# Graph layer and experts: the last token block's messages in two column halves on a bias from ScalarE, one rank product and two shared products moved

## What is computed

```python
# graph layer on the layer-normed x
HW = norm(x) @ W
x = x + relu(segment_sum(edge_w[:, None] * HW[dst], src, 1024) + bias)
# expert layer: the input is normed, then routed; 64 experts, top 2
xt = norm(x)
scores = sigmoid(xt @ Wg.T + bg)
w, idx = top_k(scores, 2);  w = w / w.sum()
nx = norm(xt)
h = silu(nx @ W1p[e] + b1p[e]) * (nx @ W3p[e] + b3p[e])     # hidden 256
y = sum over the two experts of w * (h @ W2[e] + b2[e])
z = (silu(nxs @ Ws1 + bs1) * (nxs @ Ws3 + bs3)) @ Ws2 + bs2  # shared expert, nxs = nx * gs + bs
x = x + y + z
```

## Time and profile before

| | us |
|---|---|
| median of 3 runs | 431.51 (431.15 to 432.36) |
| profiled execution | 432.0 |
| its span, first to last instruction | 430.2 |
| TensorE busy | 398.4 (93% of the span) |
| VectorE / GpSimd / ScalarE busy | 213.2 / 174.1 / 156.9 |

### The profile page before, as it was taken

The page is one execution under the profiler, slowest core; times in us unless marked ns, Lnnn a source line. Parts: engine busy times, 40 slices in busy tenths (PEclk is TensorE's granted clock), DMA queues, the critical chain, the costliest instruction groups (busy, mean ns, idle before and its releaser), DMA issues.

```text
span 430.2 us, 6405 instructions
## 1 busy us (share of the span) xinstructions
PE 398.4 (93%) x1898; PEld 207.4 (48%) x1899; DVE 213.2 (50%) x696; ACT 156.9 (36%) x387; POOL 174.1 (40%) x275
## 2 busy tenths in 40 slices
PE   6988999999999998999999999999898969897985
PEld 5656777756556557443443443443333433343331
DVE  8899998225666776633323323423313232123337
ACT  8767787322322220232332332332312321131232
POOL 2769996314655576523423323323312132121100
PEclk9999999999999998999999999999989998899999
DMA  7899971400002764499999999999999999999578
GB/s 254 211 335 408 406 287 47 137 31 26 25 25 63 281 232 146 151 402 410 400 407 405 410 406 407 406 407 406 405 406 409 405 408 404 406 399 406 231 273 325
DMA packets 44022, 129.15 MB, mean 300 GB/s; under 512 B 8054, under 2 KB 9270, under 8 KB 43858
## 3 DMA queue, kind: packets, MB, share of 16 engines
q1 hardware_dynamic: 38242, 120.45, 73.1%
q0 software_dynamic: 5744, 8.28, 5.4%
HBM read 119.64 MB, written 17.85 MB: 320 GB/s over the span
## 4 chain that ended last, share of the span: by engine, by line
PE 80%; issue 6%; DVE 5%; POOL 4%; DMA 3%; ACT 1%; SPq 1%; DVEq 0%; POOLq 0%; ACTq 0%
PE bank L1479 27%; PE bank L1342 13%; PE bank L1509 12%; PE bank L1501 5%; PE bank L1291 4%; PE bank L1467 4%; PE bank L1264 3%; DMA w<-totals 2%; PE bank L1236 2%; PE bank L1330 2%; PE bank L1363 2%; POOL M L502 1%; POOL AT L502 1%; PE bank L1351 1%; PE bank L1412 1%
## 5 line engine op out<-in xcount | busy, mean ns | idle before, releaser
L1136 DVE SCALAR_TENSOR_TENSOR osl<-bank,b13T,osl 128x64 f32<-128x64 f32 x128 | 27.5, 277 | 155.3 <-ACT osl L736 155.3
L1479 PE MATMUL bank<-w,xhT 128*64 128x512 f32 x368 | 87.6, 618 | 11.5 <-issue 11.5
L729 ACT COPY xh<-bank 128x512 f32<-128x512 f32 x33 | 19.4, 586 | 138.0 <-PE bank L1479 131.9
L1342 PE MATMUL bank<-HW,AT 128*128 128x512 f32 x128 | 58.2, 593 | 0.0
L1479 PEld LDWEIGHTS bank<-w,xhT 128*64 128x64 f32 x368 | 26.5, 141 | 56.5 <-issue 54.8
L596 POOL DMA_INDIRECT totals<-osl,A x16 | 16.4, 1028 | 80.2 <-PE bank L1467 72.1
L596 POOL DMA_INDIRECT totals<-GW,A x16 | 16.4, 1025 | 77.9 <-PE bank L1467 63.7
L1509 PE MATMUL bank<-w,osl 128*64 128x512 f32 x184 | 43.7, 593 | 1.6 <-DVE osl L1136 1.6
L592 POOL DMA_INDIRECT A<-nx_rows,A x33 | 34.3, 1039 | 12.3 <-issue 9.7
L1342 PEld LDWEIGHTS bank<-HW,AT 128*128 128x128 f32 x128 | 22.9, 191 | 21.0 <-issue 21.0
L645 ACT ACTIVATE osl<-iota,eT 128x128 f32<-128x128 f32 x90 | 27.8, 388 | 9.9 <-PE bank L1291 9.9
(11 more groups left out here) (238 smaller groups left out, 589.2 us busy)
## 6 DMA issues: line engine op xcount, KB each, us to landing
w<-in_L_ffn_W_dram SPq DMA_DIRECT2D x69, 1024.0 KB
A<-in_L_ffn_W_dram SPq DMA_DIRECT2D x15, 1024.0 KB
HW<-in_L_ffn_W_dram SPq DMA_DIRECT2D x8, 1024.0 KB
totals<-w SPq DMA_DIRECT2D x1, 4096.0 KB, 25.8
AT<-in_L_ffn_W_dram SPq DMA_DIRECT2D x4, 1024.0 KB
w<-totals SPq DMA_DIRECT2D x8, 512.0 KB, 7.4
out_dram<-X SPq DMA_DIRECT2D x8, 256.0 KB, 2.3
X<-in_x_dram SPq DMA_DIRECT2D x3, 512.0 KB, 9.5
```

Of the source, the lines that this page charges most:

```text
L1136: ins = v.scalar_tensor_tensor(hT[b][:, m, CAP * h:CAP * h + CAP], bank[4][:, (HC + m) * P + CAP * h:(HC + m) * P + CAP * h + CAP], b13T[: ...
L1342: ins = t.matmul(bank[4 + s % 2][:, :], AT[:, s % 2, k, :], HW[:, k, :], start=(k == 0), stop=(k == NB - 1))
L1479: ins = t.matmul(bank[2 + b][CAP * h:CAP * h + CAP, :], xe[b][:, c, CAP * h:CAP * h + CAP], up_w[v][:, h, :, c, :], start=(c == 0), stop=( ...
```

## The change

The messages of block 7 are summed in two column halves. ScalarE first copies the bias into the two halves of PSUM (left into bank 5, right into bank 4), and TensorE accumulates on it, all eight left half steps before the eight right ones. VectorE takes relu, sum and statistics of each half apart (`relu_add_halves`), without the bias addition, and aggregates both statistics. In `deviations` of block 7 GpSimd computes nm first and the ratio's part afterwards. The rank product of block 5 stands one `k` earlier among block 7's messages. SP reads the lists after block 5's rows instead of block 6's. Three shared products instead of four stand ahead of block 7's transposes; the fourth stands where the fifth stood, and the fifth goes behind the count, with 21 instead of 28 idle transposes after it.

```diff
@@ sync
-                if s == NB - 2:
+                if s == NB - 3:
                     for i in range(2):
                         sp.wait_ge(rec_out[i], 32 * ((DRAM_BLOCKS + 1 - i) // 2))
                     sp.dma_start(L, lists[:, :, 0:CAP * REC]).then_inc(list_in, 16)
+                if s == NB - 2:
                     sp.wait_ge(out_ps, NB)
@@ gpsimd, deviations(s)
-                g.tensor_scalar(ve[:, s, 0:1], mv1[:, s, 1:2], 1.0 + EPS, EPS * EPS, ALU.mult, ALU.add)
-                link(g.tensor_scalar(ve[:, s, 1:2], mv1[:, s, 1:2], EPS, None, ALU.add))
-                link(g.tensor_tensor(rs[:, s, :], ve[:, s, :], mhalf[:, :], ALU.pow))
+                last = s == NB - 1
+                if last:
+                    link(g.tensor_scalar(ve[:, s, 0:1], mv1[:, s, 1:2], 1.0 + EPS, EPS * EPS, ALU.mult, ALU.add))
+                    link(g.tensor_tensor(rs[:, s, 0:1], ve[:, s, 0:1], mhalf[:, 0:1], ALU.pow))
...
                 g.tensor_scalar(nm[:, s:s + 1], mv1[:, s, 0:1], rs[:, s, 0:1], -1.0, ALU.mult, ALU.mult).then_inc(nm_ready, 1)
+                if last:
+                    link(g.tensor_scalar(ve[:, s, 1:2], mv1[:, s, 1:2], EPS, None, ALU.add))
+                    link(g.tensor_tensor(rs[:, s, 1:2], ve[:, s, 1:2], mhalf[:, 0:1], ALU.pow))
@@ scalar
+            def fill_bias(half, s):
+                to, cols = message_halves[half]
+                act.wait_ge(x1_ready, s)
+                a.copy(to[:, cols], biasB[:, cols]).then_inc(bias_filled, 1)
...
+                if s == NB - 1:
+                    fill_bias(1, NB - 1)
                 if 1 <= s <= NB:
...
+                if s == NB - 2:
+                    act.wait_ge(late_in, 64)
+                    fill_bias(0, NB - 2)
@@ vector
+            def relu_add_halves(s):
+                for half, (messages, cols) in enumerate(message_halves):
+                    if half == 0:
+                        dve.wait_ge(left_ps, 1)
+                    else:
+                        dve.wait_ge(out_ps, s + 1)
+                    ins = v.scalar_tensor_tensor(X[:, s, cols], messages[:, cols], 0.0, X[:, s, cols], ALU.max, ALU.add)
+                    if half == 0:
+                        need(mark(ins))
+                    else:
+                        ins.then_inc(x1_ready, 1)
+                        dve.wait_ge(x1_ready, s + 1)
+                    c_st = mark(v.bn_stats(st12[:, 6 * half:6 * half + 6], X[:, s, cols]))
+                need(c_st)
+                v.bn_aggr(mv1[:, s, :], st12).then_inc(mv1_ready, 1)
@@ tensor
+                if s == NB - 1:
+                    for n in range(2 * ks[0], 2 * ks[-1] + 2):
+                        half, k = n // NB, n % NB
+                        messages, cols = message_halves[half]
+                        if k == 0:
+                            pe.wait_ge(bias_filled, half + 1)
+                        ins = t.matmul(messages[:, cols], AT[:, s % 2, k, :], HW[:, k, cols], start=False, stop=(k == NB - 1),
+                                       skip_group_check=True)
+                        if n == NB - 1:
+                            ins.then_inc(left_ps, 1)
...
-                    sum_messages(s, range(2, 6))
-                    rank(s - 2)
+                    if s == NB - 1:
+                        sum_messages(s, range(2, 5))
+                        rank(s - 2)
+                        sum_messages(s, range(5, 6))
+                    else:
+                        sum_messages(s, range(2, 6))
+                        rank(s - 2)
...
-            for b in range(4):
+            for b in range(3):
                 shared(b)
...
-            shared(4)
+            shared(3)
...
+            shared(4)
...
-            keep_busy(bank[0], 28)
+            keep_busy(bank[0], 21)
```

## The result

The changed kernel takes 432.95 us in the median of 20 runs (431.74 to 434.85). The kernel before, run beside it, takes 431.42 (20 runs, 430.29 to 433.35). The ratio is 1.0032, with a 95% interval of 1.002 to 1.0044. The forecast was 430.5 in a range of 429.5 to 431.6. The time lies above that range, and on the side that had been given 0.05.

A forecast was written before the change was run, and what follows sets the result against it. The prediction took the chain from block 7's messages to the first expert pair as the bound. Gains of 0.74 (GpSimd) and 0.41 (deviations), less 0.05 and 0.11, gave 0.99 us: median 431.51 to 430.5, range 429.5 to 431.6.

The forecast's parts named there:

- TensorE's end: End of block 7's messages on TensorE: stays at 154.34 us, with 0 to 0.6 us of stall kept as possible.
- VectorE: Block 7's relu and statistics: only the right half remains after the messages, ready at 155.46, a gain of 1.28 us.
- GpSimd: Block 5's scatters end earlier, freeing GpSimd: block 7's deviations begin at 156.08 instead of 156.82, a gain of 0.74 us.
- normalise: Shorter deviations save 0.41 us, so ScalarE starts normalising block 7 1.15 us earlier; three shared products end before its end.
- the list: The list of chosen experts, after block 7's routing, is ready 1.10 us earlier, at 165.76.
- the store: Block 7's stored rows, needed by the gather, land at 165.42, 0.34 us before the list; caps the gain at 1.44.
- the sum: Total gain ahead of the expert stage: 0.74 + 0.41 - 0.05 - 0.11 = 0.99 us.
- the padding: Fifth product plus 21 idle transposes before the gathered rows: 0.11 us longer, again at low clock, hiding the gather until 170.9.
- the case that I had taken for the fast one: First rival: padding at full clock or shorter in the slow stretch, so the gather decides; 429.5 us, chance 0.16.
- third rival: Low clock lasts into the expert stage's first products, costing 1.7 us per stretch: 432.2, or 433.9 with two; chance 0.07.
- one for one: Reloads follow expert products, so time saved before the first expert pair is saved at the end.
- rule on transposes: Skill's rule that transposes don't count as busy for TensorE's clock; the prediction noted the clock rose while only they ran.

The follow-up runs named there:

- after_trim_records: Changed kernel with six never-executed products (30 instructions) cut from TensorE's branch and block 6's record scatters moved behind the first four gathers: 433.87 us, ratio 1.0046.
- before_code: Kernel before with 60 waits added to a TensorE branch that never runs: 431.29 us, ratio 0.9999.
- after_again: The changed kernel measured once more, unaltered, for a second trace: 431.83 us, ratio 1.0005 to the kernel before.
- after_trim: Changed kernel with six products (30 instructions) left out of a TensorE branch that never runs: 432.35 us, ratio 1.0021.
- before_fill: Kernel before with eight idle transposes added where TensorE waits ahead of the last list product: 431.09 us, ratio 0.9989.
- before_best: Kernel before with the sixth buffer's weight loads behind block 7's store and eight idle transposes ahead of the last list product: 432.98 us, ratio 1.0031.
- after_best_again: Changed kernel, repeat run, with sixth buffer's weight loads behind block 7's store, 12 idle transposes ahead of the last list product, 28 in the padding: 430.73 us, ratio 0.997.
- after_list_old: Changed kernel with the read of the lists put back one block later, behind block 6's rows: 433.08 us, ratio 1.0022.

## Why the prediction was wrong, by its own steps

**Right: TensorE's end.** Forecast 154.34 with no stall; 154.16 by TensorE's last product. The right half's bias was copied at 148.94 to 149.31, before it was wanted.

**Right: VectorE.** Forecast 0.42 + 0.42 + 0.19 and a gain of 1.28 us. The rows have 0.42, 0.43 and 0.21, and the statistics are ready at 155.33, 1.14 us after the end of the messages instead of 2.38: a gain of 1.24.

**Right, and too small: GpSimd.** The first scatter of block 5 starts at 153.04 (forecast 153.40), the second takes 0.96 us. It did so in all the changed kernels, where those with the old order had 1.16 to 1.33. So the Trainium skill's rule ("SBUF — State Buffer", section "SBUF: two separate sides"), which I had set at even odds with the single row, is borne out in this number. The deviations begin at 155.50 instead of 156.08, 1.31 us after the end of the messages instead of 2.46: a gain of 1.15 us, forecast 0.74. GpSimd still comes last, but barely. The chain leads through its scatter, which ended at 155.42, 0.08 us before the deviations; VectorE's aggregation ended 0.17 us before them, where the kernel before needed 0.08 us from VectorE's end (156.74) to the deviations (156.82). So about 0.1 us of VectorE's gain lies idle, and not the 0.5 that the prediction had set aside.

**Right, and too small: normalise.** From the start of the deviations to ScalarE's takes 1.25 us instead of 1.77: 0.52 less, forecast 0.41. ScalarE starts 2.56 us after the messages' end, 4.23 before: 1.67 us less, forecast 1.15. The three shared products end at 157.74 and the normalised rows at 157.56, so taking the fourth away was needed.

**Right in size, by two errors: the list.** 11.19 us after the messages' end, 12.27 before: 1.08 us, forecast 1.10. The 0.5 us that ScalarE gained beyond the forecast was lost again at L1060, which held VectorE for 1.14 us; in after_trim_records, where it took 0.22, the list comes 10.54 us after the end of the messages, 0.65 earlier.

**Wrong: the store.** The step that failed is the one on the landing of block 7's rows, put at 165.42, which "caps the gain at 1.44, and costs nothing below". It took a time that had been read at one issue (159.42, 6.0 us) as a fixed landing, set by loads ahead of it that don't move. For the bulk of the store that held: fourteen sixteenths were down by 165.51, the fifteenth at 165.74. But a store has landed only with its last sixteenth, and that came at 167.76, 2.3 us later than forecast. The change lengthens TensorE's code, and its fetch moved from 167.0, behind the store, to 162.0, into it; before_code shows that such a move alone can make the last sixteenth late. In after_again and after_trim several sixteenths are late, as it seems by block 6's earlier scatters on the same DMA engines. A gather 0.97 us behind the last sixteenth starts at 168.73 instead of 166.91: 1.8 us, against a gain of 0.99 in the sum. In the sum the store stood with the price 0 and 0.34 us in hand; a rival in which a transfer decides was missing, and the range was too narrow for it.

**Wrong: the padding.** Expected was the low clock over it once more, "hidden behind the padding's end". In the first trace it was so (3.70 us, and a wait of 1.15 behind). In others it ran at full clock, the case that I had taken for the fast one, with the time 429.5. It is the bad one while the gather is late: the padding ends early, TensorE stands, and the low clock comes under the products. That is the third rival's mechanism, priced at 1.7 us and seen at 1.6 and 2.2 in two of the nine traces of changed kernels without added transposes ahead of the list; 0.07 was too little for it.

**Right: one for one.** A time gained or lost ahead of the first reload is found again at the end, to within 1.4 us in all traces.

**Left open.** The two measurements of the changed kernel, 1.5 and 0.5 us above before, are not split into store and clock: only one execution of each has a trace. That block 6's scatters are what makes several sixteenths late rests on one trace, and why a fetch that holds a DMA engine for 1 us can make a sixteenth 2 us late, or not late at all (before_fill), no run shows.

## What to carry to other kernels

A transfer's landing is not a fixed time: work out anew what is on the DMA engines while it is under way, count the engines' own code fetches, which move when code is added even where it never runs, and remember that it is complete only with its slowest sixteenth. When a chain is brought forward, look at every second condition of its last step, and put the transfer that is waited for ahead of the loads that can wait. In four traces the low clock fell under dense products behind an idle place of TensorE, and cost 1.4 to 2.9 us. Idle transposes helped together with the change and the earlier store, and not without the change (before_best).

## What the runs showed of the hardware

- **A fetch of code can delay data.** One 16 KB packet on the instruction queue takes 0.9 to 1.7 us (1.0 in the changed kernel), and in ten traces in which it met the 256 KB store the last sixteenth landed 1.1 to 2.2 us later than the one before it. In two others, before_fill and after_best_again, it was late by no more than 0.25 us. Where the fetch falls depends on the length of code that never runs: 60 instructions moved it by 4.7 us (167.0 to 162.3).
- **A long jump had a price:** 2.15 us of TensorE with 452 more instructions to jump over, nothing seen with 60.
- **GpSimd can hold VectorE up, too.** L1060 scales two columns by a third, all in SBUF, in 0.22 us; beside GpSimd's scatter and the operation behind it (163.13 to 163.75) it took 1.14 and ended at 163.78. With those scatters moved it took 0.22 in both kernels that had this. It also took 0.22 in after_list_old, where it began 0.28 us into the scatter and not 0.50; what decides between the two is not shown. The section on SBUF of the Trainium skill, cited above, calls the lock exclusive and held for the whole of an instruction. The end at 163.78 fits that; L1058, with both inputs in SBUF, does not: it began 0.36 us into the same scatter and took its usual 0.23.
- **Transposes and the clock.** The granted clock went from 0.50 to 1.00 while only idle transposes ran, at 170.2 us before and at 169.8 after. With eight or twelve of them ahead of the list's last product no low clock followed in four of five traces, where it did in all twelve without. Neither fits the rule on transposes of the Trainium skill that the prediction cited.
